# A GNN layer and a mixture of experts on one core: the expert products change their number kinds

## What is computed

```python
x = x + gnn(layernorm(x), edges, ...)
xg = layernorm(x).reshape(-1, 512)[token_ids]           # rows sorted by expert
for e in range(8):
    h = gelu(xg @ w1[e], approximate=False)              # 512 -> 256
    y = where(bin_ids == e, h @ w2[e], y)                # 256 -> 512
out = zeros((512, 512)).at[token_ids].add(w * y)
x = x + out
```

## Time and profile before

| | |
|---|---|
| three runs, median | 164.88 us (164.72 to 165.08) |
| the profiled execution | 164.8 us, its span 163.1 us |
| mean granted clock of TensorE | 0.988 |
| PE, PEld busy | 146.3 us (90%), 96.7 us (59%) |
| DVE, ACT, POOL busy | 119.6, 82.6, 34.9 us (73, 51, 21%) |
| chain that ended last, by engine | PE 61%, DVE 19%, issue 5%, POOL 4%, DMA 4% |

### The profile page before, as it was taken

One profiled execution on the slowest core, in us unless ns is written; L12 is line 12 of the kernel. 1 busy time (PEld: TensorE's weight loads), 2 busy tenths in 40 slices (PEclk: granted clock), 3 DMA queues, 4 the chain that ended last, 5 costly groups with the idle time before them and its releaser, 6 DMA issues.

```text
span 163.1 us, 3502 instructions
## 1 busy us (share of the span) xinstructions
PE 146.3 (90%) x1130; PEld 96.7 (59%) x1133; DVE 119.6 (73%) x300; ACT 82.6 (51%) x210; POOL 34.9 (21%) x55
## 2 busy tenths in 40 slices
PE   2978899999999999999999999998999999999800
PEld 1436677878889855746844445543777873777100
DVE  1899999999999969898567758899567745443300
ACT  3268667777777785302421615995354333533100
POOL 7310000000000000000000600047700876173650
PEclk9999999999999999999999999999999999999995
DMA  3999999999000000000000000424698598547585
GB/s 89 264 380 288 275 373 371 367 368 312 17 0 4 2 4 4 2 0 4 0 0 0 0 4 0 171 88 129 201 326 310 112 196 191 72 53 91 78 115 64
DMA packets 15354, 21.71 MB, mean 133 GB/s; under 512 B 2942, under 2 KB 7808, under 8 KB 15332
## 3 DMA queue, kind: packets, MB, share of 16 engines
q1 hardware_dynamic: 12994, 16.02, 29.3%
q0 software_dynamic: 2240, 5.24, 17.7%
q10 hardware_dynamic: 98, 0.17, 0.3%
HBM read 15.19 MB, written 6.23 MB: 131 GB/s over the span
## 4 chain that ended last, share of the span: by engine, by line
PE 61%; DVE 19%; issue 5%; POOL 4%; DMA 4%; ACT 1%; POOLq 1%; DVEq 0%
DVE ring L749 11%; PE bank L1670 10%; PE bank L1549 10%; PE bank L1887 7%; PE bank L1875 6%; PE bank L1524 4%; PE bank L1878 4%; DMA ring<-x_rows,from_i 2%; PE bank L1848 2%; POOL ring L656 2%; PE bank L1470 2%; PE bank L1808 2%; PE bank L1514 2%; DVE stats L1085 2%; DVE x_sb L1079 2%
## 5 line engine op out<-in xcount | busy, mean ns | idle before, releaser
L1549 PE MATMUL bank<-ring 128*128 128x110 bf16 x324 | 30.0, 222 | 3.7 <-DVE ring L749 2.3
L749 DVE TENSOR_TENSOR ring<-iota_slots,lo 128x1024 bf16<-128x1024 f16 (+1 forms) x41 | 27.4, 669 | 0.0
L1549 PEld LDWEIGHTS bank<-ring 128*128 128x128 bf16 x324 | 19.7, 98 | 11.6 <-issue 5.9
L1261 ACT CAST at<-bank 128x400 f32 (+1 forms) x41 | 20.6, 502 | 7.5 <-PE bank L1555 6.6
L749 DVE TENSOR_TENSOR ring<-iota_dst,key 128x880 bf16<-128x880 f16 (+1 forms) x41 | 24.4, 595 | 0.0
L653 POOL CAST at_r<-ew 128x1024 fp32r<-128x1024 f32 x2 | 2.6, 1328 | 82.6 <-PE bank L1799 82.6
L667 POOL DMA_INDIRECT out<-at,to_i x10 | 15.7, 1572 | 20.7 <-DMA out<-x_sb 8.0
L1782 PE MATMUL bank<-wd3t_sb,at 128*128 128x512 f32 x40 | 17.7, 592 | 0.0
L1670 PE MATMUL bank<-at,ring 128*128 128x512 bf16 (+1 forms) x89 | 16.8, 343 | 0.1
L656 POOL DMA_INDIRECT ring<-x_rows,from_i x10 | 11.4, 1135 | 17.3 <-DMA x_rows<-at 14.5
L1887 PE MATMUL bank<-ew,at 128*128 128x512 f32 x32 | 14.9, 594 | 0.0
(11 more groups left out here) (223 smaller groups left out, 246.5 us busy)
## 6 DMA issues: line engine op xcount, KB each, us to landing
ew<-in_w SPq DMA_DIRECT2D x16, 512.0 KB, 9.5
x_sb<-in_x SPq DMA_DIRECT2D x9, 256.0 KB, 5.4
out<-x_sb SPq DMA_DIRECT2D x9, 256.0 KB, 4.1
wd3t_sb<-in_Wd3T SPq DMA_DIRECT2D x1, 512.0 KB, 4.8
x_rows<-xn SPq DMA_DIRECT2D x1, 512.0 KB, 2.8
x_rows<-at SPq DMA_DIRECT2D x1, 512.0 KB, 2.8
w1t_sb<-in_W1T SPq DMA_DIRECT2D x1, 256.0 KB, 5.0
bd_sb<-in_bd SPq DMA_DIRECT2D x1, 256.0 KB, 4.1
```

The lines of the kernel that those rows point to most:

```text
L749: last = v.tensor_tensor(hot[:, slot, 0:tiles].rearrange("p t (n a) -> p t n a", a=2), lanes[:, 0:n].rearrange("p (n a) -> p n a", a=2).un ...
L1261: nc.scalar.copy(at[:, :, bass.ds(column, wide)], bank[j][:, 0:CH * wide].rearrange("p (c n) -> p c n", c=CH)).then_inc(s_placed, 1)
L1549: last = mm(to, hot_src[:, j, t], hot_dst[:, j, t], start=(t == 0 and not ends), stop=(first and t == tiles - 1), skip_group_check=not ends)
```

## The change

Products up are made in native fp32: eight products of 160 columns from the whole rows and the whole weights, into one bank for each expert (of_up: bank 2 or 3 by turns), both halves m side by side. No parts of w1 or of the gathered rows are made; the rows are copied out of PSUM as they are, bank 0 and the tails by ACT, bank 1 by DVE. ACT takes the GELU straight from PSUM. Products down are made by `product`, six fp32r products of 512 columns, from two parts of the hidden features (first part ACT, second part DVE) and two parts of w2 (first part ACT, six before the first copy of rows and two in the loop; second part DVE). POOL makes no parts any more on this path. The tail products down (L1899) stay in native fp32. s_up_sp counts once for each product up where it counted twice, and SP's waits follow. Cut to its core:

```diff
+        by_w2 = [at_r[:, o * w2_len:(o + 1) * w2_len] for o in range(2 * W_HI)]
-        xg_t = xnt_r[:, 2 * NP:2 * NP + 4 * KD * SLOTS].rearrange("p (b k h t) -> p b k h t", b=2, h=2, k=KD)
+        xg_t = xnt_flat[:, 2 * NP:2 * NP + 2 * KD * SLOTS].rearrange("p (b k t) -> p b k t", b=2, k=KD)
...
+        def of_up(e):
+            return bank[2 + e % 2][:, 0:KF * SLOTS].rearrange("p (k t) -> p k t", k=KF)
...
-                    sp.wait_ge(s_up_sp, c - TC + 2)
+                    sp.wait_ge(s_up_sp, (c - TC + 3) // 2)
...
-            for e in range(2):
-                nc.gpsimd.tensor_copy(w1_first[e], weights(e)[0]).then_inc(s_whi, 1)
...
-                if TC - 1 <= c <= TC:
-                    weight_rest_of(c - TC + 1, 0)
+                def keep_gathered(e):
+                    if e >= 2:
+                        dve.wait_ge(s_up_sp, e - 1)
+                    dve.wait_ge(s_xgT, 2 * e + 2)
+                    v.tensor_copy(xg_t[:, e % 2, 2:4, 0:P],
+                                  bank[1][:, 0:2 * P].rearrange("p (k t) -> p k t", k=2)).then_inc(s_xg_dve, 1)
+                def second_part(e):
+                    dve.wait_ge(s_w2_first, e + 1)
...
+                    v.tensor_tensor(w2_second[e], weights(e)[1], w2_first[e].bitcast(F32), ALU.subtract).then_inc(s_w2_second, 1)
+                def second_hidden(e):
+                    dve.wait_ge(s_hs, e + 1)
+                    v.tensor_tensor(hs[:, e % 2, 1], hs_raw[:, :, :], hs[:, e % 2, 0].bitcast(F32),
+                                    ALU.subtract).then_inc(s_hs_second, 1)
                 for c in range(TC + 2, CH - 1):
-                    up_rest(c - TC)
                     sum_rows(c)
+                    if c >= TC + 3:
+                        second_part(c - TC - 3)
                 dve.wait_ge(s_slot_weight, 1)
-                gathered_rest(0)
+                keep_gathered(0)
                 sum_rows(CH - 1)
-                gathered_rest(1)
-                sum_hidden(0)
+                keep_gathered(1)
                 for e in range(NE):
-                    if e + TC + 1 < NE:
-                        up_rest(e + TC + 1)
                     if e >= 1:
                         keep_results(e - 1)
+                    second_hidden(e)
                     if e + 2 < NE:
-                        gathered_rest(e + 2)
-                    if e + 1 < NE:
-                        sum_hidden(e + 1)
+                        keep_gathered(e + 2)
+                        second_part(e + 2)
...
+                def finish_tails(e):
+                    q = e % TEAM * MORE
+                    nc.scalar.activation(hs_tail[:, e // TEAM, :, q:q + MORE], of_up(e)[:, :, P:], ACT.Gelu).then_inc(s_hs_tail, 1)
+                def first_part(e):
+                    if e >= 6:
+                        act.wait_ge(s_down_sp, e - 5)
+                    nc.scalar.copy(w2_first[e], weights(e)[1]).then_inc(s_w2_first, 1)
+                def finish_hidden(e):
+                    act.wait_ge(s_up_sp, e + 1)
                     if e >= 1:
+                        act.wait_ge(s_hs_second, e)
+                    nc.scalar.activation(hs_raw[:, :, :], of_up(e)[:, :, 0:P], ACT.Gelu).then_inc(s_hs_raw, 1)
+                def first_hidden(e):
+                    act.wait_ge(s_hs_raw, e + 1)
...
+                    nc.scalar.copy(hs[:, e % 2, 0], hs_raw[:, :, :]).then_inc(s_hs, 1)
                 for e in range(NE):
+                    finish_hidden(e)
+                    finish_tails(e)
+                    first_hidden(e)
                     if e + 2 < NE:
                         keep_gathered(e + 2)
-                    if e + 1 < NE:
-                        keep_part(e + 1)
+                    if e + 4 in (6, 7):
+                        first_part(e + 4)
...
                 def up_slots(e):
+                    pe.wait_ge(s_xg_act, 2 * (e + 1))
+                    pe.wait_ge(s_xg_dve, e + 1)
+                    if e >= 2:
+                        pe.wait_ge(s_hs_raw, e - 1)
+                        pe.wait_ge(s_hs_tail, e - 1)
                     for m in range(KF):
                         for k in range(KD):
-                            mm(acc[:, 0:2 * SLOTS], w1_hi[:, k, m * P:(m + 1) * P],
-                               xg_t[:, e % 2, k].rearrange("p h t -> p (h t)"), start=(k == 0), stop=False)
-                        for k in range(KD):
-                            last = mm(acc[:, 0:SLOTS], w1_lo[:, e, k, m * P:(m + 1) * P], xg_t[:, e % 2, k, 0],
-                                      start=False, stop=(k == KD - 1))
+                            last = mm(of_up(e)[:, m], ew1[:, e, k, m * P:(m + 1) * P], xg_t[:, e % 2, k], start=(k == 0),
+                                      stop=(k == KD - 1))
                 def down_slots(e):
-                    pe.wait_ge(s_hs, e + 1)
+                    pe.wait_ge(s_hs_second, e + 1)
+                    pe.wait_ge(s_w2_second, e + 1)
-                    for k in range(KF):
-                        last = mm(bank[4 + 2 * (e % 2)][:, 0:D], hs[:, e % 2, k], ew2[:, e, k], start=(k == 0),
-                                  stop=(k == KF - 1))
+                    product(bank[4 + 2 * (e % 2)][:, 0:D], lambda h, k: hs[:, e % 2, h, k],
+                            lambda h, k: (w2_lo if h else w2_hi)[:, k], KF).then_inc(s_down_sp, 1)
```

More of the change, by code:

```diff
@@ L230, in gnn_moe @@
         hs_at = (XG + TEAMS) * D
-        hs_raw = ring_flat[:, hs_at:hs_at + KF * SLOTS].rearrange("p (k t) -> p k t", k=KF)
-        hs_part = ring_flat[:, hs_at + KF * SLOTS:hs_at + 2 * KF * SLOTS].rearrange("p (k t) -> p k t", k=KF)
+        hs_raw = ring_flat[:, hs_at:hs_at + KF * P].rearrange("p (k t) -> p k t", k=KF)
         hs_tail = ring_flat[:, hs_at + 2 * KF * SLOTS:hs_at + 2 * KF * SLOTS + TEAMS * KF * P].rearrange(
             "p (g k t) -> p g k t", g=TEAMS, k=KF)
-        hs = at2_flat[:, 4 * NP:4 * NP + 2 * KF * P].rearrange("p (b k t) -> p b k t", b=2, k=KF)
-        w1_first += [xnt_r[:, o * w1_len:(o + 1) * w1_len] for o in range(2)]
+        hs = at2_r[:, 4 * NP:4 * NP + 4 * KF * P].rearrange("p (b h k t) -> p b h k t", b=2, h=2, k=KF)
+        w2_first = by_w2[0:4] + [xnt_r[:, o * w2_len:(o + 1) * w2_len] for o in range(2)] + by_w2[0:2]
+        w2_second = (by_w2[4:6] + [at2_r[:, 4 * D + o * w2_len:4 * D + (o + 1) * w2_len] for o in range(2)]
+                     + [ew1_r[:, o * w1_len:(o + 1) * w1_len] for o in range(4)])
         x2_more = at2_flat[:, 3 * NP:3 * NP + 2 * D].rearrange("p (b n) -> p b n", b=2)
@@ L704, in _ @@
             with pool.If(dense != 0):
-                for e in range(2):
-                    nc.gpsimd.tensor_copy(weights_hi(e)[1], weights(e)[1]).then_inc(s_whi, 1)
-                for e in range(2, NE):
+                pool.wait_ge(s_ew, 16 * 2 * NE)
+                pool.wait_ge(s_agg2, len(SPANS))
+                for e in range(NE):
                     if e >= W_HI:
@@ L1045, in _ @@
             add_bias(CH - 1, CH)
-            def weight_rest_of(e, i):
-                dve.wait_ge(s_whi, 2 * i + e + 1 if e < 2 else 2 * (e + 1))
-                lo = down_lo(e) if i else up_lo(e)
-                v.tensor_tensor(lo, weights(e)[i], weights_hi(e)[i].bitcast(F32), ALU.subtract).then_inc(s_wlo, 1)
             def weights_rest(e):
-                for i in range(2):
-                    weight_rest_of(e, i)
-            def up_rest(e):
-                dve.wait_ge(s_whi_act, e - 1)
-                v.tensor_tensor(up_lo(e), weights(e)[0], w1_first[e].bitcast(F32), ALU.subtract).then_inc(s_wlo_up, 1)
+                dve.wait_ge(s_whi, 2 * (e + 1))
+                for lo, w, hi in zip((up_lo(e), down_lo(e)), weights(e), weights_hi(e)):
+                    v.tensor_tensor(lo, w, hi.bitcast(F32), ALU.subtract).then_inc(s_wlo, 1)
             def hidden_rest(i):
@@ L1398, in keep_gathered @@
                     if e >= 2:
-                        act.wait_ge(s_up_sp, KF * (e - 1))
-                    for i in range(2):
-                        act.wait_ge(s_xgT, 2 * e + i + 1)
-                        nc.scalar.copy(xg_t[:, e % 2, 2 * i:2 * i + 2, 0, 0:P],
-                                       bank[i][:, 0:2 * P].rearrange("p (k t) -> p k t", k=2)).then_inc(s_xg_hi, 1)
-                    act.wait_ge(s_tailT, e // TEAM + 1)
-                    if e >= 1:
-                        act.wait_ge(s_xg_lo, 3 * e)
@@ L1407, in keep_gathered @@
-                    nc.scalar.copy(xg_t[:, e % 2, :, 0, P:], of_tails(e)).then_inc(s_xg_hi, 1)
-                def first_part(e):
-                    nc.scalar.copy(w1_first[e], weights(e)[0]).then_inc(s_whi_act, 1)
-                def keep_part(e):
-                    for m in range(KF):
-                        act.wait_ge(s_up_sp, KF * e + m + 1)
-                        if e >= 1:
-                            act.wait_ge(s_hs_sum, KF * (e - 1) + m + 1)
```

(20 more changed lines are left out.)

64 lines of the change are left out of this document (17 added, 47 removed).

## The result

The changed kernel takes 163.02 us (median of 4 runs, 162.34 to 163.18) against 164.86 for the kernel before on the same chip: ratio 0.987 (95% interval 0.985 to 0.989). The prediction was 162.9 us. The profiled execution took 162.87, with a span of 161.0 against 163.1.

A forecast was written before the change was run, and what follows sets the result against it. The prediction took TensorE's chain of expert products, from the first gather's landing to the end of down 6, as the bound. Its terms, +0.96 - 2.17 - 0.75 = -1.96 us, took 164.88 to 162.9 us, range 161.6 to 165.6.

The forecast's parts named there:

- U: Product up of one expert on TensorE: from 2.11 to 2.23 us, +0.12 each, +0.96 us for eight.
- the change of kind: Switch between kinds of product on TensorE: 0.05 us counted in each product up and each product down.
- T: Transposes of one expert's gathered rows on TensorE: 0.44 us, claimed not to change.
- D: Product down of one expert on TensorE: from 1.77 to 1.46 us, -0.31 each, -2.17 us for seven.
- Rivals 2, 3 and 4: Records of 160 columns at 0.147: 164.3 us (0.12); fp32r without 22 ns: 162.1 (0.10); weight loads pace U: 169.7 (0.13).
- The start: First gathers on POOL, no longer held up by DVE's two-input subtractions, let TensorE start earlier: -0.75 us, ends 0 and -0.9.
- Rival 1: POOL's long gathers are the first of their kind, not DVE's doing, so no earlier start: 163.7 us, chance 0.17.
- The tail: End of down 6 to the end stays 12.6 us; 1.25 us stall before down 7 hidden behind add 6's landing: cost 0.
- S: Theory of a later run: how long after add 6 the next add starts sets how long add 6 takes to land.
- Slack of gather 5: Gather 5 on POOL starts at 128.45, lands at 131.7, needed at 132.9: slack 1.2 us or more, no cost.

The follow-up runs named there:

- experiment 3: Changed kernel with products down back in native fp32, two of 512 columns from whole weights, no parts of hidden features: 164.33 us, 0.997 against the kernel before.
- experiment 4: Changed kernel with DVE's second parts 0 and 1 of w2 moved ahead of the sums of chunks 6 and 7, beside the gathers: 163.71 us, 0.995.
- experiment 2: Changed kernel with unused 0.69 us bn_stats on DVE between down 7 and the scaling of result 7: two of them 163.23 us, one 163.10 us.
- experiment 5: Changed kernel with unused DVE instructions added ahead of the sums of chunks 6 and 7: with two SBUF inputs 163.63 us, with one 162.91 us.
- the second part first: Changed kernel, but for the last expert DVE makes the second part of hidden 7 before scaling result 6: 162.43 us (0.988), again 161.81 us (0.976).
- add 6 late: Changed kernel with some 0.9 us of POOL's own unused work ahead of scatter-add 6: 162.30 us, 0.981 against the kernel before.
- add 7 late: Kernel making hidden 7's second part before scaling result 6, plus some 0.9 us of POOL's own unused work ahead of scatter-add 7: 162.16 us, 0.980.
- experiment 6: Changed kernel with twelve fp32r products of 256 columns per product down in place of six of 512: 164.04 us.

## Why the prediction was right

- **U** (+0.12 each): 2.17 against 2.11, half of it. The records take 2.17 / 16 = 0.136 as taken; the 0.05 for the change of kind doesn't appear in U.
- **T** (no change): 0.36 against 0.44 from start to start, but only because the first record of D starts earlier and is longer. Counted by ends, the chain of waits has T 0.44, U 2.17 and D 1.40, which is 4.01 in all. The kind of product changes twice in each expert, as before, now into D and back into U. The prediction put 0.05 for it into U and 0.05 into D; no cost is left to see in either.
- **D** (-0.31 each): 1.49 against 1.77, -0.28. Six records of 0.233 (0.235 taken) are 1.40; the other 0.09 is what T is shorter by. An expert is 4.02 where the terms gave 4.13, and the stretch lost 1.62 us, not 1.21. Rivals 2, 3 and 4 fall with the records at 0.136 and 0.233. That D brings most of the gain is shown by experiment 3. The Trainium skill (TensorE: Matmul & The Clock Gate, section Back-to-back issue gap) has 0.216 at 512 columns by its formula for a single warm product; the rows disagree.
- **The start** (-0.75): -1.13, and 0.7 of it goes again in experiment 4. Gathers 0 and 1 take 1.14 and 0.96 (1.1 and 0.95 said), and T stands without idle time. One sentence of the step was off: gather 1 was to land 3.2 us after its start, the old 3.69 less what POOL was held up; it takes 3.6, and starts earlier instead (110.61 against 110.95). In the profile with one bn_stats of experiment 2, the same up to the last expert, the first T still waits 0.36 us for the landing of gather 0, so this idle time is gone with little to spare. Rival 1 falls: experiment 4 brings the long gathers back with the same DVE work in another place, and experiment 5 shows on one gather that two SBUF inputs do it and one doesn't. The Trainium skill (SBUF — State Buffer, section Who interferes with whom) names this contention, and the trace agrees. Its inference that a tensor_tensor spares descriptor generation would leave the gathers as they are; they take 1.26 to 1.47 us against 0.96. Which part of a gather waits, no run here tells.
- **The tail** (0): +1.15, the term that was mis-sized. The mechanism of the step was right: a stall of 1.18 before down 7 (1.25 said), add 7 later by 1.0 (0.8 said) and clear of POOL, the last add waiting for the landing of add 6. What failed is the sentence that this landing stays at its time: it came 1.0 later behind add 6. With the second part first the tail, from the end of down 6 to the end, is 12.7 and 12.6 us in the two profiles (13.7 and 13.2 in the changed kernel); with add 6 late it is 12.8. So an early add 7 is worth 0.5 to 1.1 us, and the 13.7 of the profiled execution is at the unlucky end. Why add 6 lands late in some executions, and only where add 7 comes late, stays open: add 5 and the kernel with add 7 late speak against S.
- **Slack of gather 5** (1.2 said): too much. In the changed kernel gather 5 starts earlier than said (127.35 against 128.45) but lands 4.2 us after its start, at 131.5, where the prediction took 3.2; T(5) stands at 131.76, 0.2 behind the landing. In experiment 6 the gather starts 1.3 later and lands after 4.7, and T(5) waits 1.20 for it.

By its terms the span was to lose 1.96; it lost 1.13 + 1.62 - 1.15 = 1.60, and 0.4 more by the early decode3. The number 162.9 was met with luck: two gains that were underrated (0.4 each) and a cost that was missed (1.15) nearly cancel, and in the profiled execution the early decode3 makes up the rest.
